# ScalarE makes the large pass of the quantisation of h, VectorE only its row factors

## The reference

```python
x = x + tanh(g_xattn) * attention(layernorm(x), ctx, seg_id, ...)   # 16 heads of 128 + 64 (rope) columns
x = x + tanh(g_ffn) * ffn(layernorm(x), w1, b1, ln_g, ln_b, w2, b2)

def act_quant(x):                       # per row
    scale = 127.0 / clip(max(abs(x)), 1e-05)
    return clip(round(x * scale), -128, 127) / scale
def bitlinear158(x, w, b):
    return act_quant(rms_norm(x)) @ weight_quant(w).T + b     # weights rounded to -1, 0, 1 times a mean
def ffn(x, ...):
    h = silu(bitlinear158(x, w1, b1))   # 256 -> 1024
    h = gelu(h)
    h = layer_norm(h, ln_g, ln_b)
    return bitlinear158(h, w2, b2)      # 1024 -> 256
```

## Time and profile before

| | |
|---|---|
| runs | 227.37 us median of 3 (227.22 to 228.9) |
| profiled execution, its own time | 226.34 us |
| its span, first to last instruction | 224.5 us |
| mean granted TensorE clock | 0.927 of full speed |
| busy: PE / DVE / ACT / POOL | 180.4 / 175.6 / 148.5 / 144.3 us |
| DMA moved | 20.89 MB, most of it before 65 us |

### The profile page before, as it was taken

The page is one execution under the profiler, slowest core; times in us unless marked ns, Lnnn a source line. Parts: engine busy times, 40 slices in busy tenths (PEclk is TensorE's granted clock), DMA queues, the critical chain, the costliest instruction groups (busy, mean ns, idle before and its releaser), DMA issues.

```text
span 224.5 us, 4128 instructions
## 1 busy us (share of the span) xinstructions
PE 180.4 (80%) x1224; PEld 137.4 (61%) x1224; DVE 175.6 (78%) x373; ACT 148.5 (66%) x444; POOL 144.3 (64%) x198
## 2 busy tenths in 40 slices
PE   1499777989998999699999989998998986850413
PEld 0377565767885865677778858776885852620211
DVE  2346677744889599789999999999999988969740
ACT  3412055579486996788699699879969997724130
POOL 0233475264289289967986996898698799374440
PEclk9999699999999999799999999999999999975555
DMA  5984968962421111011202111120212100000001
GB/s 94 303 252 101 372 207 267 318 219 90 140 96 47 47 48 65 34 47 51 104 12 96 48 70 51 47 105 14 93 48 74 48 0 23 0 25 1 23 3 34
DMA packets 10860, 20.89 MB, mean 93 GB/s; under 512 B 1936, under 2 KB 4176, under 8 KB 10576
## 3 DMA queue, kind: packets, MB, share of 16 engines
q1 hardware_dynamic: 10176, 19.70, 26.4%
q10 hardware_dynamic: 656, 0.86, 1.6%
HBM read 11.11 MB, written 1.05 MB: 54 GB/s over the span
## 4 chain that ended last, share of the span: by engine, by line
POOL 28%; PE 23%; DVE 18%; issue 17%; DMA 7%; ACT 4%; SPq 2%; ACTq 1%; DVEq 0%; POOLq 0%
POOL turn_room L497 7%; POOL prob_room L591 5%; PE bank_pair L940 4%; DMA crossed<-turn_room 4%; PE bank_ff L1033 4%; DVE turn_room L1267 3%; DMA wkr<-in_wkr 3%; POOL x_small L521 3%; POOL x_deq L558 3%; POOL x_small L547 3%; POOL x_all L575 2%; DVE z L1342 2%; PE bank_score L995 2%; POOL h_small L521 2%; PE bank_ff L886 2%
## 5 line engine op out<-in xcount | busy, mean ns | idle before, releaser
L792 ACT ACTIVATE prob_room<-bank_score,neg_max 128x128 f32<-128x128 f32 x128 | 45.4, 371 | 17.0 <-DVE neg_max L1420 17.0
L497 POOL TENSOR_TENSOR turn_room<-turn_room,crossed 128x512 f32<-128x512 f32 x32 | 40.7, 1272 | 15.5 <-DMA crossed<-turn_room 14.6
L591 POOL TENSOR_TENSOR prob_room<-prob_room,rsum 128x512 f32<-128x512 f32 x32 | 34.3, 1072 | 17.1 <-DVE rsum L1428 17.1
L1267 DVE TENSOR_TENSOR turn_room<-bank_pair,cst 128x1024 f32<-128x1024 f32 x32 | 38.7, 1210 | 7.5 <-PE bank_pair L940 7.4
L940 PE MATMUL bank_pair<-qcT,wcat 96*128 96x128 f32 x256 | 35.9, 285 | 1.6 <-DVE wcat L1254 1.1
L995 PEld LDWEIGHTS bank_score<-kcat,turn_room 128*128 128x128 f32 x256 | 34.6, 196 | 1.8
L940 PEld LDWEIGHTS bank_pair<-qcT,wcat 96*128 96x128 f32 x256 | 32.1, 197 | 4.9 <-DVE wcat L1254 2.6
L995 PE MATMUL bank_score<-kcat,turn_room 128*128 128x128 f32 x256 | 34.6, 279 | 0.0
L792 ACT ACTIVATION_READ_ACCUMULATOR prob_room<-bank_score,neg_max 128x1 f32 x128 | 26.7, 209 | 0.0
L780 ACT COPY probT_room<-bank_prob 128x512 f32<-128x512 f32 x32 | 18.7, 586 | 12.0 <-PE bank_prob L1007 10.9
L1007 PE MATMUL bank_prob<-cst,prob_room 128*128 128x128 f32 x128 | 20.1, 280 | 6.8 <-POOL prob_room L591 6.8
(11 more groups left out here) (130 smaller groups left out, 365.1 us busy)
## 6 DMA issues: line engine op xcount, KB each, us to landing
crossed<-turn_room SPq DMA_DIRECT2D x64, 128.0 KB, 2.1
wmo<-in_wmo SPq DMA_DIRECT2D x4, 640.0 KB, 5.7
w_sb<-in_w SPq DMA_DIRECT2D x2, 1024.0 KB, 8.3
wfold<-in_wfold SPq DMA_DIRECT2D x4, 320.0 KB, 9.6
x_all<-in_x SPq DMA_DIRECT2D x4, 256.0 KB, 6.0
out_x<-y SPq DMA_DIRECT2D x8, 128.0 KB, 1.7
ctx_rest<-in_ctx_rest SPq DMA_DIRECT2D x2, 384.0 KB, 8.2
cst<-in_consts ACTq DMA_DIRECT2D x1, 512.0 KB, 9.5
```

Source lines behind the costliest of these rows:

```text
L497: nc.gpsimd.tensor_tensor(qcat[:, k, :, :, :], qcat[:, k, :, :, :], crossed[:, k % 2, :, :, :], ALU.add).then_inc(pair_done, 1)
L591: nc.gpsimd.tensor_tensor(p, p, rsum[:, k % 2, :].unsqueeze(2).broadcast_to([P, GROUP, kts * P]), ALU.mult).then_inc(prob_scaled, 1)
L792: last = nc.scalar.activation(prob_of(n, kts)[:, j, :], src[:, j, :], ACT.Exp, bias=neg_max[:, k % 2, j:j + 1], accum_out=esum[:, k % 2, j ...
L1267: nc.vector.tensor_tensor(both, pair.unsqueeze(1).broadcast_to([P, 2, 2, 2 * P]), tables[:, f % TILES, :, :].unsqueeze(2).broadcast_to([P, ...
```

## The change

The pass over the 1024 columns of h moves to ScalarE, as an activation with a scale per row and a constant bias (the new `quantise_h` of ScalarE, behind the exponentials of step 2). VectorE keeps the two row factors (`scale_for_h`) and raises a new semaphore `h_steps`; it also waits until ScalarE has read the factor of the tile before. The orders of all four engines within a body are written anew, and the output of a tile moves from the last step of one body to the first step of the next (`OUT_STEP, OUT_LAG`). No other operation is added or taken away.

```diff
-OUT_STEP, OUT_LAG = 3, 3
+OUT_STEP, OUT_LAG = 0, 4
+            def quantise_h(c):                                   # ScalarE
+                act.wait_ge(h_steps, c + 1)
+                nc.scalar.activation(h[:, slot(c), :], h[:, slot(c), :], ACT.Copy, scale=hs(QMUL),
+                                     bias=MAGIC + LIFT).then_inc(hq_ready, 1)
-            def quantise_h(c):                                   # VectorE
-                if c >= 1:
-                    dve.wait_ge(h_deq_ready, c)
-                quantise(h[:, slot(c), :], hs, h_amax[c], h_floor, h_scale, c + 1, hq_ready)
+            def scale_for_h(c):
+                dve.wait_ge(h_floor, c + 1)
+                dve.wait_ge(dve_link, h_amax[c])
+                if c >= 1:
+                    dve.wait_ge(h_deq_ready, c)
+                    dve.wait_ge(hq_ready, c)
+                nc.vector.tensor_scalar(hs(YMAX), hs(AMAX), 1.0 / QMAX, hs(FLOOR), ALU.mult, ALU.max).then_inc(h_scale, 1)
+                dve.wait_ge(h_scale, c + 1)
+                nc.vector.reciprocal(hs(QMUL), hs(YMAX)).then_inc(h_steps, 1)
```

More of the change, by code:

```diff
@@ L297, in build @@
         h_scale = sem("h_scale")
+        h_steps = sem("h_steps")
         h_deq_ready = sem("h_deq_ready")
@@ L617, in body @@
                     invert_h(f - 3)
-                if there(f, 3):
-                    dequantise_h(f - 3)
+                if n + 1 < B:
+                    input_root(n + 1)
+                k, n = 1, step_no(f, 1)
                 if 1 <= n < N + 1:
@@ L625, in body @@
                     input_root(n + 1)
-                k, n = 3, step_no(f, 3)
+                k, n = 2, step_no(f, 2)
+                if 1 <= n < N + 1:
+                    normalise(*behind(f, k, 1), kts)
+                if n + 1 < N:
+                    add_rope_step(*ahead(f, k, 1))
                 if there(f, 2):
@@ L825, in body @@
                         copy_probT(*behind(f, k, lag), kts)
+                    if there(f, 2):
+                        tanh(f - 2, 0)
+                    if there(f, 2):
+                        tanh(f - 2, 1)
                     if 2 <= n < B + 1:
@@ L1092, in body @@
                     k, n = 0, step_no(f, 0)
-                    if there(f, 4):
-                        down(f - 4)
-                    if n + AHEAD < N:
-                        project(*ahead(f, k))
                     if n == 0:
@@ L1110, in body @@
                     if there(f, 2):
-                        up(f - 2)
+                        transpose_x(f - 2)
+                    if n + AHEAD < N:
+                        project(*ahead(f, k))
                     if lag <= n < N + lag:
@@ L1115, in body @@
                     k, n = 1, step_no(f, 1)
+                    if n + AHEAD < N:
+                        project(*ahead(f, k))
+                    if there(f, 2):
+                        up(f - 2)
+                    if lag <= n < N + lag:
+                        transpose_probs(*behind(f, k, lag), kts)
                     if n == 0:
@@ L1143, in body @@
                         transpose_inputs(n - 1)
-                    if lag <= n < N + lag:
-                        transpose_probs(*behind(f, k, lag), kts)
-                    if n + AHEAD < N:
-                        project(*ahead(f, k))
                     if there(f, 1):
@@ L1445, in body @@
                     k, n = 0, step_no(f, 0)
+                    if 1 <= n < N + 1:
+                        invert_sums(*behind(f, k, 1))
+                    if n < N:
+                        softmax_max(f, k, kts)
+                    if there(f, 4):
+                        output(f - 4)
+                    if there(f, 3):
+                        absmax_h(f - 3)
                     if n + AHEAD < N:
                         turn_step(*ahead(f, k))
[L1448 to L1453 removed]
+                    if there(f, 2):
+                        first_product(f - 2, 0)
                     prepare(f, k)
                     k, n = 1, step_no(f, 1)
[L1456 to L1457 removed]
                     if 1 <= n < N + 1:
@@ L1465, in body @@
                         silu(f - 2, 0)
-                    if there(f, 3):
-                        absmax_h(f - 3)
                     if n + AHEAD < N:
@@ L1501, in body @@
                         quantise_x(f - 1)
-                    if there(f, 3):
-                        output(f - 3)
+                    if there(f, 2):
+                        scale_h(f - 2)
                     prepare(f, k)
```

91 lines of the change are left out of this document (38 added, 53 removed).

## The result

The changed kernel takes **232.61 us** (median of 3, 232.5 to 233.26), where before took 227.37: a ratio of 1.022, 95% interval 1.0145 to 1.0291. It is slower, by 1.4 to 2.9%; the forecast was 224.6, faster. The profiled execution took 232.61 us for a span of 230.8, against 226.34 for 224.5. The page after, to be read against the earlier trace rows: less work on VectorE (172.7 us instead of 175.6) and more on ScalarE (155.2 instead of 148.5), as planned, in a longer span.

A forecast was written before the change was run, and what follows sets the result against it. GpSimd's and VectorE's parts of one loop and VectorE's own work were taken as bounds, TensorE close behind, then slowest after the change. Terms summed to -2.75 us: 223.6 profiled, 224.6 as median, range 221.5 to 227.8.

The forecast's parts named there:

- The full tile: Steady tiles between starts of `residual`: 19.3 to 19.5 us, taken as 19.4, or -0.25 a tile over three tiles.
- the loop through TensorE: From `residual`'s release through a new gap of about 0.7 us before step 0's scores: 19.5 us a tile.
- R(6) to R(7): Between the `residual` starts of tiles 6 and 7: later `x_deq` against earlier attention output, +0.2 us.
- The start: Up to tile 0's `residual`: first scores ahead of step 2's projection delay its rotation, +0.5 us, bounds 0 and +1.5.
- VectorE alone has 18.75: VectorE's own work in a full tile after the change: 19.65 less 0.2 idle and 0.70 for the pass.
- the sum: Full tile's loop: GpSimd's part, grown for normalise and blocking to 11.25, plus VectorE's 8.02, gives 19.27 us.
- R(1) to R(2): Between `residual` starts of tiles 1 and 2: shorter VectorE part against GpSimd's growth, -0.7 us, bounds -1.5 and 0.
- Rival C: TensorE's clock halves behind the new gap before step 0's scores: +6.8 us, 231.4 in all; chance 0.08.
- one tile only: Case within Rival C: the clock falls in a single tile, 226.3 us in all.
- R(0) to R(1): Between `residual` starts of tiles 0 and 1: second weight's rounding falls between both `first_product`, +0.7 us, bounds -0.5 and +1.
- R(4) to R(6): From tile 4's `residual` start to tile 6's: a full tile at -0.25, then one without a projection at -0.2 us.
- Run-out: After tile 7's `residual`: last `first_product` to last transposes shortens from 14.65 to 12.1 us, -2.5, bounds -3.2 and -1.0.

The follow-up runs named there:

- mask_ahead: three_mended with the scores' wait for rotated queries moved behind the mask's matmul; a full tile went from 19.46 to 19.31 us.
- bias_early: The changed kernel with GpSimd's one-time scaling of the bias row moved to its idle time; R(1) to R(2) fell by 4.86 us to 19.17.
- three_mended: The changed kernel with the edits of weights_moved, bias_early and turn_before_absmax together; ratio 0.978 to the kernel before.
- run_out: three_mended with four single calls on GpSimd and VectorE behind the last residual in other places; ratio 0.974 to the kernel before.
- weights_moved: The changed kernel with second-weight rounding one step earlier and ScalarE's copy two steps later; R(0) to R(1) fell by 3.2 us to 18.72.
- turn_before_absmax: The changed kernel with VectorE's rotation of step 2 ahead of absmax_h; the two slow tiles took 19.47 and 19.26 us instead of 20.72 and 20.78.
- before_mask: The kernel before the change, with the scores' wait for rotated queries behind the mask's matmul; ratio 0.993, full tiles unchanged at 19.63 us.
- fetch_shift: The changed kernel with 15 small matmuls at TensorE's start to shift its instruction fetches; one slow tile instead of two, total time not given.
- order_only: The changed kernel's orders with VectorE making the pass over h again, at the place of its row factors; ratio 1.055 to the kernel before.
- all_mended: three_mended with the edits of run_out and mask_ahead together; ratio 0.970 to the kernel before.

## Why the prediction was wrong

**What held.** The full tile: 19.45 and 19.50 for a forecast of 19.3 to 19.5, the loop through TensorE with its new gap before the scores of step 0 (0.81 and 0.87 for 0.7), `x_deq` at 0.34 and `h_deq` at 1.30, VectorE busy for 18.7 (18.4). ScalarE's pass took 1.15 (1.06) and nobody waited in full tiles.

**What only looks right.** R(6) to R(7) came +0.23 for +0.2, in part by luck: it took 14.8 to 14.9 in the three profiles with a hit of step 2 just ahead of it, and 15.14 (+0.5) in the five with neither a hit there nor a fall of the clock. The start came -0.53 where +0.5 was forecast (bounds 0 and +1.5); R(0) lies up to 4 us apart over the profiles, so one profile of each tells nothing about that term.

**What was mis-sized within it.** "VectorE alone has 18.75" left out that `scale_h` takes 2.06 when GpSimd's normalise blocks it, though the text named that blocking a few lines earlier and charged it in the sum to GpSimd alone. With it the sum is 18.75 + 0.58 = 19.33, and mask_ahead shows VectorE's loop at 19.3. Its wait before `first_product` was released by `up`, not `x_deq`.

**Step that failed: R(1) to R(2), "the shorter VectorE part gives -1.8 less the 1.1", -0.7, measured +2.6.** The interval was never walked; a steady tile's difference was put on one that has work of its own (and GpSimd's growth was 1.1 in this term where the loop's sum had 1.44). The scaling of 0.48 in front of the first bias add now stood ahead of a normalise that TensorE waits for, pushed it beside `scale_h`, and made a gap of 2.01. Rival C had the mechanism (a clock that falls behind a gap), but tied it to the rope in every full tile and gave "one tile only" no weight of its own. bias_early shows it: 4.9 us. An estimate of the parts: the gap shrank by 1.64 us, and 6.8 us of half clock, at the 1.6 us that 3.4 us of it cost between three_mended and run_out, make 3.2. The same price fits the other profiles with that gap (3.4 us less of it: -1.6 in weights_moved; 3.4 us more: +1.4 in turn_before_absmax). So how much of the 4.9 an execution pays depends on the clock as well, and a run without the long gap can also pay some (1.6 in three_mended).

**Step that failed: R(0) to R(1), "+0.7, bounds -0.5 and +1", measured +2.3.** The rounding was seen between the two `first_product`, but its 2.5 us were netted against a gain on ScalarE that didn't come, since the weight copy still stood ahead of the table load. weights_moved shows 3.2 us for the two pieces, more than the whole difference to before.

**Step that was missing: the crossing of step 2.** The prediction lists what moves on each engine, but VectorE's rotation of step 2, now behind the output and `absmax_h`, was not followed through SP's queue to its landing. In before such a hit (the fetch of 170.9) cost a rope wait of 0.74 but no time (R(5) to R(6) took 18.53, as in before_mask, which has no hit there); after, the chain runs through it and pays 1.3 and 1.5 us (20.72 and 20.78 against 19.47 and 19.26). turn_before_absmax and fetch_shift show it. R(4) to R(6) measured +3.3 where -0.45 was forecast; the two hits are 2.8 of it. Whether a fetch meets a crossing is luck of the program's length; that the crossing had no slack is not.

**Run-out, -2.5 forecast, -1.3 measured.** From the last `first_product` to the last transposes it took 12.38 for 12.1. What failed is that `first_product` was taken to start as before; R(7) to there took 8.42 instead of 7.42, since `up` needs the bank of the output of tile 5, which stood behind `scale_h`. run_out takes 1.1 back.

**Open.** Why R(5) to R(7) stays 1.3 us above before in run_out without a hit (19.28 + 15.14 against 18.53 + 14.62), and what decides the clock between the same gaps.

## What to carry to other kernels

A new order of work has to be walked through each stretch that isn't a steady tile, with every one-time instruction in it: here 4.9 of the 8.2 us lost lay in two intervals with some 5 us of one-time work, and moving four calls (two of them of the weights) made the same change 2.2% faster than before. When a producer moves later, follow it through its transfers to the landing and ask how late the slowest landing in the profile would be, not the median one. Where two loops lie 0.15 us apart, taking 0.37 from one brings 0.15. When two profiles differ in a stretch, read the granted clock of both there first: equal lengths hid different clocks (order_only), and an interval that seemed unexplained was one (all_mended).
